# DLRM interaction tower on one Trainium2 core: transposes as ordinary fp32 matmuls with the identity

## The reference

```python
e = jnp.stack([tbl_0[ids[:, 0]], ..., tbl_31[ids[:, 31]]], axis=1)   # 512, 32, 256
iu, ju = jnp.triu_indices(32, k=1)
z = jnp.einsum('bnd,bmd->bnm', e, e)[:, iu, ju]
h = jnp.concatenate([z, dense_ctx], axis=1)                           # 512, 512
h = jnp.maximum(h @ W_top1 + b_top1, 0.0)                             # 512, 512
h = jnp.maximum(h @ W_top2 + b_top2, 0.0)                             # 512, 256
y = h @ W_top3                                                        # 512, 1
```

## Time and profile before

| | us |
|---|---|
| median of 3 runs | 251.21 (251.07 to 251.59) |
| span of the profiled execution, first to last instruction | 251.4 |
| PE matmuls busy | 166.6 (66%) in 2544 records |
| PE weight loads busy | 113.4 (45%) |
| DVE busy | 69.8 (28%) |
| ACT busy | 57.1 (23%) |
| POOL busy | 121.6 (48%) |
| mean granted TensorE clock | 0.756 of full |

### The profile page before, as it was taken

The page is one execution under the profiler, slowest core; times in us unless marked ns, Lnnn a source line. Parts: engine busy times, 40 slices in busy tenths (PEclk is TensorE's granted clock), DMA queues, the critical chain, the costliest instruction groups (busy, mean ns, idle before and its releaser), DMA issues.

```text
span 251.4 us, 6104 instructions
## 1 busy us (share of the span) xinstructions
PE 166.6 (66%) x2544; PEld 113.4 (45%) x2544; DVE 69.8 (28%) x253; ACT 57.1 (23%) x193; POOL 121.6 (48%) x132
## 2 busy tenths in 40 slices
PE   0431076666667994766667995666665974779976
PEld 0211043333335962433335973333333952447765
DVE  0000014151515025151515015151515014244331
ACT  2000003131313113131313113131313123134231
POOL 4777365556566155656666146666565235600000
PEclk9999999999999996555555597555555596555989
DMA  5833223222322112322322112222222112200000
GB/s 138 286 105 106 76 70 94 83 80 85 87 85 83 38 51 80 92 82 83 85 81 82 42 42 83 83 83 83 81 83 89 44 42 85 86 23 3 4 0 0
DMA packets 7766, 18.91 MB, mean 75 GB/s; under 512 B 2593, under 2 KB 3489, under 8 KB 7618
## 3 DMA queue, kind: packets, MB, share of 16 engines
q0 software_dynamic: 6144, 16.79, 22.9%
q1 hardware_dynamic: 1602, 1.84, 2.4%
HBM read 18.62 MB, written 0.00 MB: 74 GB/s over the span
## 4 chain that ended last, share of the span: by engine, by line
PE 63%; DVE 18%; another core or an unknown queue 7%; issue 6%; DMA 3%; ACT 2%; POOL 0%; DVEq 0%; ACTq 0%
PE xt_ps L274 28%; PE gram_ps L287 19%; PE mlp_ps L306 9%; DVE z L183 9%; DVE xt L175 7%; PE mlp_ps L317 4%; PE mlp_ps L297 2%; DMA rows<-in_table,row_number 2%; DVE slots L193 1%; ACT xt L175 1%; ACT slots L238 1%; DMA ids_sb<-in_ids 1%; POOL rows L165 0%; PE mlp_ps L325 0%
## 5 line engine op out<-in xcount | busy, mean ns | idle before, releaser
L165 POOL DMA_INDIRECT rows<-in_table,row_number x128 | 121.4, 948 | 98.6 <-PE xt_ps L274 68.1
L287 PE MATMUL gram_ps<-xt 128*32 128x32 f32 x2048 | 57.6, 238 | 68.1 <-DVE xt L175 50.6
L287 PEld LDWEIGHTS gram_ps<-xt 128*32 128x32 f32 x2048 | 40.7, 142 | 110.2 <-DVE xt L175 59.8
L274 PE MATMUL xt_ps<-identity,rows 128*128 128x128 f32 x256 | 81.9, 418 | 12.8 <-DMA rows<-in_table,row_number 9.8
L175 DVE COPY xt<-xt_ps 128x256 f32<-128x256 f32 x64 | 27.2, 425 | 156.7 <-PE xt_ps L274 136.8
L175 ACT COPY xt<-xt_ps 128x256 f32<-128x256 f32 x64 | 23.9, 373 | 121.1 <-PE xt_ps L274 89.2
L274 PEld LDWEIGHTS xt_ps<-identity,rows 128*128 128x128 f32 x256 | 35.6, 191 | 21.4 <-issue 12.8
L183 DVE COPY z<-slots 32x32 f32<-32x32 f32 x160 | 34.2, 214 | 2.5
L183 ACT COPY z<-slots 32x32 f32<-32x32 f32 x96 | 23.4, 244 | 4.3 <-DVE slots L193 2.9
L306 PE MATMUL mlp_ps<-z,w1z_sb 128*128 128x128 f32 x128 | 23.1, 364 | 1.9 <-DVE z L183 1.9
L306 PEld LDWEIGHTS mlp_ps<-z,w1z_sb 128*128 128x128 f32 x128 | 22.4, 276 | 2.7 <-issue 2.7
(11 more groups left out here) (6 smaller groups left out, 1.8 us busy)
## 6 DMA issues: line engine op xcount, KB each, us to landing
rows<-in_table,row_number POOLq DMA_INDIRECT x128
w1z_sb<-in_w1z SPq DMA_DIRECT2D x1, 1024.0 KB, 5.0
w_sb<-in_w SPq DMA_DIRECT2D x1, 512.0 KB
ids_sb<-in_ids SPq DMA_DIRECT2D x1, 64.5 KB, 1.8
identity<-in_eye SPq DMA_DIRECT2D x1, 64.0 KB, 1.9
upper_sb<-in_takes_upper SPq DMA_DIRECT2D x1, 64.0 KB, 1.9
ctx_sb<-in_ctx_t SPq DMA_DIRECT2D x1, 32.0 KB
w1c_sb<-in_w1c SPq DMA_DIRECT2D x1, 32.0 KB
```

What stands on the lines that cost most here:

```text
L165: nc.gpsimd.indirect_dma_start(rows[:, n % SLOTS, :], None, table, bass.IndirectOffsetOnAxis(ap=row_number[:, n:n + 1], axis=0),).then_inc ...
L274: last = nc.tensor.transpose(xt_ps[g % 2][:, k, :], rows[:, g % SLOTS, k * P:(k + 1) * P], identity[:])
L287: last = nc.tensor.matmul(gram_ps[u % 2][F * j:F * j + F, g % UNIT, :], x, x, start=(k == 0), stop=(k == KD - 1))
```

## The change

In `transposes` (L269 to L276), the two blocks of a group are produced by ordinary matmuls with the rows as the stationary operand and the identity as the moving one, each starting and ending its own accumulation, instead of by the transpose mode with the same two operands. The results land in the same PSUM tiles, and the same last instruction raises `rows_transposed`. Nothing else differs.

```diff
@@ -271,8 +271,8 @@
                     pe.wait_ge(xt_ready[g % 2], t * (G // 2) + g // 2)
                 pe.wait_ge(rows_landed[g % SLOTS], t * (G // SLOTS * 16) + (g // SLOTS + 1) * 16)
                 for k in range(KD):
-                    last = nc.tensor.transpose(xt_ps[g % 2][:, k, :], rows[:, g % SLOTS, k * P:(k + 1) * P],
-                                               identity[:])
+                    last = nc.tensor.matmul(xt_ps[g % 2][:, k, :], rows[:, g % SLOTS, k * P:(k + 1) * P],
+                                            identity[:], start=True, stop=True)
                 last.then_inc(rows_transposed, 1)
```

## The result

The changed kernel takes **255.49 us** (median of 4 runs, 255.35 to 255.57) against 251.14 for the kernel before (250.95 to 251.59): ratio 1.0174, 95% interval 1.0144 to 1.0205. It is slower where I had forecast 244.5 us. Medians in this document are over all runs; ratios and their intervals leave out runs over 1.5% above the fastest of the same kernel.

What follows compares the result with a forecast made beforehand. Steady stretches were taken as bound by a loop of gathers and late completions, PE by itself at the layer stages and the end. -9.4 + 2.6 - 0.8 - 0.9 + 1.3 + 0.2 = -7.0 gave 244.5 us, range 241 to 260.

Steps and rivals of the forecast that it cites:

- Term 4: Three layer stages: entered at 2.4 GHz, L297 and L306 save 9.4 us together; packed groups there cost 2.6.
- rival B: Clock level swings in the laps; perhaps two thirds of the layer stages' saving remain: 248 us, 245 to 252; chance 0.18.
- Term 2: Duration of a group's transposes on PE: 0.44 us added at 1.2 GHz, 0.22 at 2.4.
- Term 3: Steady laps, some 110 groups: PE needs 2.90 of 3.12 us a lap at 1.2 GHz, so cost nothing.
- Rival C: Late completions change rhythm in the laps, groups go singly: +4 to +10 us, about 252 to 264; chance 0.06.
- Term 5: The end, at 2.4 GHz: six groups -0.8, L317's first eight -0.9, six more groups +1.3, last L306 0 us.
- Term 6: The beginning: the first group's transposes stand in the open, +0.2 to +0.5 us; up to 31 us otherwise 0.
- Rival A: Clock stays as it is, PE only gets more work where packed: +7.4, 258.8 us, 256 to 262; chance 0.26.

Runs made afterwards that it cites:

- e1: The changed kernel, unchanged, run again on a chip with late completions: 259.28 us, ratio 1.0262 to the kernel before.
- e9: The changed kernel once more, on a chip with late completions: 258.30 us, ratio 1.0252 to the kernel before.
- e4: Kernel before with only the first of each group's two blocks transposed by an ordinary matmul: 259.61 us, ratio 1.0247.
- e12: Kernel before plus two extra ordinary matmuls a group in the eight groups ahead of each layer stage, late completions: 248.23 us, ratio 0.9846.
- e10: Kernel before with plain DMAs in place of the gathers, on a chip with late completions: 191.24 us, ratio 0.7581.
- e11: Changed kernel with plain DMAs in place of the gathers, on a chip with late completions: 179.47 us, ratio 0.7115 to the kernel before.
- e3: Kernel before with ordinary-matmul transposes only in groups 0 to 8 of the later quarters and from group 22 of the last: 255.78 us, ratio 1.0120.
- e7: Changed kernel with plain DMAs in place of the gathers, on a chip without late completions: 182.51 us; kernel before with the same DMAs 190.84.
- e14: Kernel before with ordinary-matmul transposes only from group 9 on in the first three quarters, no late completions: 194.69 us, ratio 0.9706.
- e18: e14 again, in another batch without late completions: 194.45 us, ratio 0.9733 to the kernel before.
- e17: The changed kernel once more, on a chip without late completions: 195.61 us against 197.47 for the kernel before.
- e8: Kernel before plus two extra ordinary matmuls a group in the eight groups ahead of each layer stage, no late completions: 192.68 us, ratio 0.9689.
- e16: e12 plus extra matmuls in groups 18 to 21 of the last quarter and eight ahead of the last L306, no late completions: 189.70 us, ratio 0.9547.
- e13: The kernel before, profiled again on a chip without late completions: 197.79 us.
- e5: The kernel before, profiled a second time, on a chip without late completions: 194.86 us.

## Why the prediction was wrong

**Term 4 failed: "the layer stages find it there".** The forecast took it that the level, once up, would hold through laps with PE busy 1.74 of 3.12 us. No row showed that: the earlier trace rows has a fall at 1.48 of 3.30 us and none at 3.27 of 3.40. It did not hold: at 45.4 to 52.2 PE was busy 4.80 of 6.80 us at 2.4 GHz, and the clock fell; at 52.3 to 62.4 it was busy 9.29 of 10.10 us at 1.2 GHz, and the clock rose. Faster work makes the idle time that loses the level, slower work fills it. How soon the level comes back is not regular: from 69.3 to 86.3 PE was busy 16.98 of 17.00 us, and the clock stayed at 0.50. What I called rival B, the swing, is what happened. I gave it two thirds of the saving, as if a stage met either level by the share of time. In the profile none of three stages was met at the upper level, in e1 and e9 one each. So -9.4 became 0 in the first (L306's three together gave 0.7 us), and the stages, where packed groups now ran in part at 1.2 GHz, got 1.3, 1.0 and 0.9 us longer instead. How that splits is open, since e4 loses about as much there with half the work. The size of the gain itself was nearly right: 2.1 to 2.7 us a stage measured (e12, with its added work paid), 3.1 forecast.

**The evidence on the clock** was weaker than the prediction read it. PE full for 3.40 us at a granted 0.50 was to show that transpose mode doesn't raise the level; but the changed kernel, with ordinary matmuls, was full from 214.4 to 226.3 (11.90 of 11.90 us) before it rose. The conclusion held all the same, by e10 against e11. The "eight ordinary matmuls" at 230.69 are eight records, four matmuls.

**Term 2** was right in kind, 512 records and three steps for one, and low in size. Spans of 1.22 and 0.71 us against 0.69 and 0.44 make +0.53 and +0.27 a group, for 0.44 and 0.22; my upper ends had been 0.52 and 0.29. The middle value spread a longer first step (0.38 us, then 0.21 each, in L317's first eight) over seven, where a group has three.

**Term 3** held, on the profile: 37.8 us for groups 44 to 68, 38.1 before. PE at 1.2 GHz needs 3.10 of 3.12 us a lap, not 2.90, so nothing is left over; that half-lap losses came with it in e1 and e9 fits, but is not shown: e3, whose laps stayed in transpose mode up to group 96, has one too, and e4, with a shorter lap on PE, has none and is no faster. Rival C, a slower rhythm of the copies, did not come either: 28 groups took 44.0 us, 45.6 before.

**Term 5.** The end's saving came: the clock was up from 226.3 on. But eight groups before it (214.73 to 225.56) ran packed at 1.2 GHz, 1.55 us each, and "six groups at 0.87" were six at 0.93; from group 108 on nothing was lost or gained (37.5 us in both) where -0.4 net was forecast. The last L306 took 5.25 us for 5.44.

**Term 6.** Up to group 8 the cost was 1.2 us, not 0.2 (36.0 to 37.2), and the next laps gave 1.6 back.

**The baseline** was wrong by 2 us: I took the profiled execution to lie 0.2 us from the median. Its span must have 1.8 added. The relative sum is unharmed; the comparison of the profiles is not, and shows only 2.1 of 4.3 us. Where the rest is can't be read, for no profile of a typical execution of the kernel before on such a chip exists.

**Range and chances.** 255.5 lies inside 241 to 260, but by luck: the upper part of the range stood for rivals A and C, and neither is what happened. The direction had 0.33. Rival A's price of +7.4 was not paid, since the clock was up for part of the time; A's ground (0.50 in the laps) is also not what was seen. The Trainium skill's rule for transposes (Perfetto Trace Analysis, Optimizing Tensor Performance, Transposes), to do them in transpose mode, is right for this kernel on the recorded chip, 1.7%; e10 and e11 are a case where the measurement goes against it, by 6%.

## What to carry to other kernels

Transposes by ordinary fp32 matmuls cost twice the records, and pay by what they do to TensorE's clock. They paid most where their density kept it at 2.4 GHz nearly throughout (4 to 6%, e7 and e11). With gathers but no late completions they paid little: at most 3% in part of the groups (e14, e18), nothing clear in all of them (e17). With late completions they lost: the clock rose when PE was slow and full, and fell again when it was fast. If a packed stretch of matmuls is entered at 1.2 GHz, a few ordinary matmuls put into the idle time just ahead of it are cheaper than changing the work everywhere: they gained 1.5% here (e12), 3% on the other sort of chip (e8) and 4.5% there with the end included (e16). And a profile's span is not its time: compare spans with spans.

## What the hardware showed that I had not expected

**One program, two speeds by the chip.** The kernel before had medians of 251.1 to 252.7 us in three series, two of them on chip 8 (the first one's chip is not on record), and of 197.5 to 198.3 in three others, on chips 9, 14 and 10. So the sort went with the chip where one came twice; more than that is not shown. Of the 55 us between the first profile and e13's, 17.5 lie before group 8 and 30.2 in the three stretches of laps of the table, where the late completions are: 1.56 us from the end of a transpose to the start of its copy at 54.82, against 0.04 us. The cause is open. It needs the gathers (e10), and not every chip has it (e5, e13).

**Late where gathers come in pairs.** In the changed kernel, on the chip with late completions, there is a stretch where PE is the bound and each gather stands alone:

```profile
214.73 1.22 PE L274 MATMUL xt_ps<-identity,rows 128*128 128x128 f32 x4
...
216.06 0.42 DVE L175 COPY xt<-xt_ps 128x256 f32<-128x256 f32 x1 [1.78 <-PE xt_ps L274]
216.23 0.94 POOL L165 DMA_INDIRECT rows<-in_table,row_number  x1 [1.06 <-PE xt_ps L274]
...
217.60 0.37 ACT L175 COPY xt<-xt_ps 128x256 f32<-128x256 f32 x1 [3.19 <-PE xt_ps L274]
217.78 0.94 POOL L165 DMA_INDIRECT rows<-in_table,row_number  x1 [0.61 <-PE xt_ps L274]
```

Transposes end at 215.95 and the copy starts at 216.06; POOL has 0.6 us between gathers. The same profile shows it in two more such stretches (100 to 106 and 159 to 165 us), with 0.04 us from transposes to copy. In the laps two gathers are 0.30 us apart, and completions that fall into the second or just behind it come late. Which makes the other is open, since POOL waits for the same completions: gathers may come in pairs because completions do. And on the other sort of chip gathers 0.30 us apart went with no delay (e13). Whether spacing the gathers out would free the kernel before of the delay was not tried.
